# Two cross-attention layers over 16 sequences on one core: turning every probability tile in blocks, with SBUF-to-SBUF exchanges

## The reference

```python
# layer 0: 16 heads of 64
q = x @ Wq + bq;  k = ctx @ Wk + bk;  v = ctx @ Wv + bv
x = layernorm(softmax(q k^T / 8, masked) v @ Wo + bo + x)
# layer 1: 16 heads of 16, self-attention, cross-attention, feed-forward
x = layernorm(x + attention(x q_w, x k_w, x v_w) o_w + o_b)
x = layernorm(x + attention(x cq_w, ctx ck_w, ctx cv_w) co_w + co_b)
x = layernorm(x + relu(x lin1_w + b) lin2_w + b)      # 256 -> 1024 -> 256
```

## Time and profile before

| | before |
|---|---|
| median of 3 runs | 1821.75 us |
| the profiled execution: its own time / its span | 1826.15 / 1824.3 us |
| ScalarE busy | 1190.3 us, 65% |
| GpSimd busy | 990.9 us, 54% |
| data moved by DMA | 324.12 MB, 178 GB/s on average |

### The profile page before, as it was taken

One profiled execution on the slowest core, in us unless ns is written; L12 is line 12 of the kernel. 1 busy time (PEld: TensorE's weight loads), 2 busy tenths in 40 slices (PEclk: granted clock), 3 DMA queues, 4 the chain that ended last, 5 costly groups with the idle time before them and its releaser, 6 DMA issues.

```text
span 1824.3 us, 36986 instructions
## 1 busy us (share of the span) xinstructions
PE 1719.5 (94%) x11328; PEld 1287.7 (71%) x11328; DVE 1269.6 (70%) x4778; ACT 1190.3 (65%) x3985; POOL 990.9 (54%) x1030
## 2 busy tenths in 40 slices
PE   7999999999999999999999999999999999998887
PEld 5776677777777677777777777677777777776556
DVE  3465667786868668686776868678686867667763
ACT  3364766667676666767666676766667677566752
POOL 3252655657465464746556474555657565455742
PEclk9999999999999999999999999999999999998899
DMA  7432327585766758576585757658575766613010
GB/s 167 143 106 84 107 67 230 172 273 161 238 204 200 245 170 272 161 244 206 178 266 181 249 159 236 209 181 280 173 251 163 226 223 182 202 59 139 30 58 12
DMA packets 227521, 324.12 MB, mean 178 GB/s; under 512 B 31744, under 2 KB 196352, under 8 KB 219136
## 3 DMA queue, kind: packets, MB, share of 16 engines
q1 hardware_dynamic: 224208, 321.75, 55.5%
q10 hardware_dynamic: 3120, 0.01, 0.1%
HBM read 170.69 MB, written 151.00 MB: 176 GB/s over the span
## 4 chain that ended last, share of the span: by engine, by line
PE 77%; DVE 6%; DMA 5%; ACT 5%; SPq 5%; issue 2%; POOL 0%; POOLq 0%; DVEq 0%
PE ps_g L681 45%; PE ps_t L824 10%; PE ps_t L847 8%; PE ps_s L800 8%; ACT prob L930 3%; PE ps_av L800 3%; DMA prob_b<-p_kept 3%; PE ps_av L847 3%; DVE prob L1105 2%; DMA p_kept<-blocks 2%; SPq L593 1%; PE ps_g L687 1%; DVE res_ln L1081 1%; DVE prob_b L1136 1%; SPq L576 1%
## 5 line engine op out<-in xcount | busy, mean ns | idle before, releaser
L1229 POOL TENSOR_TENSOR prob<-prob,recip 128x512 f32<-128x512 f32 x768 | 788.4, 1049 | 670.5 <-DVE recip L1115 670.4
L930 ACT ACTIVATE prob<-prob,ext 128x256 f32<-128x256 f32 x1536 | 757.2, 499 | 11.7 <-DVE ext L1105 11.5
L940 ACT ACTIVATE prob_t<-ps_t 128x512 f32<-128x512 f32 x384 | 226.3, 594 | 398.1 <-PE ps_t L824 397.3
L824 PE MATMUL ps_t<-ident,prob 128*128 128x128 f32 x1920 | 304.6, 283 | 7.6 <-DVE prob_b L1136 5.4
L930 ACT ACTIVATION_READ_ACCUMULATOR prob<-prob,ext 128x1 f32 x1536 | 295.5, 192 | 0.0
L824 PEld LDWEIGHTS ps_t<-ident,prob 128*128 128x128 f32 x1920 | 216.9, 142 | 94.2 <-issue 51.6
L1105 DVE CUSTOM_DVE_ANT_0 prob<-ps_s,mask_a 128x256 f32<-128x256 f32 x392 | 145.3, 421 | 88.3 <-PE ps_s L800 70.6
L1127 DVE STREAM_TRANSPOSE blocks<-prob 128x512 f32<-128x512 f32 x288 | 183.9, 676 | 3.2 <-POOL prob L1229 2.3
L1105 DVE CUSTOM_DVE_ANT_0 prob<-ps_s,zero 128x256 f32<-128x256 f32 x392 | 144.4, 418 | 45.3 <-PE ps_av L800 37.3
L1105 DVE CUSTOM_DVE_ANT_0 prob<-ps_s,mask_b 128x256 f32<-128x256 f32 x368 | 135.9, 417 | 24.5 <-PE ps_s L800 14.8
L800 PE MATMUL ps_s<-k_ctx,q 64*128 64x256 f32 x784 | 144.8, 402 | 7.3 <-DVE ext L1105 3.0
(11 more groups left out here) (116 smaller groups left out, 2980.9 us busy)
## 6 DMA issues: line engine op xcount, KB each, us to landing
p_kept<-blocks SPq DMA_DIRECT2D x576, 128.0 KB, 2.4
prob_b<-p_kept SPq DMA_DIRECT2D x144, 512.0 KB, 3.4
k_parts_C<-k_hl SPq DMA_DIRECT2D x64, 256.0 KB, 3.1
k_parts_B<-k_hl SPq DMA_DIRECT2D x64, 256.0 KB, 3.1
q_parts_B<-q_hl SPq DMA_DIRECT2D x64, 256.0 KB, 3.5
k_B<-k_parts_B SPq DMA_DIRECT2D x16, 1024.0 KB, 7.6
q_B<-q_parts_B SPq DMA_DIRECT2D x16, 1024.0 KB, 7.7
q_parts_C<-k_hl SPq DMA_DIRECT2D x64, 256.0 KB, 4.7
```

Of the source, the lines that this page charges most:

```text
L824: last = nc.tensor.transpose(two(ps_t[e])[:, kt, qt * P:(qt + 1) * P], src[:, e, qt, kt * P:(kt + 1) * P], ident[:, :])
L930: last = nc.scalar.activation(tile, tile, ACT.Exp, bias=ext[:, slot, e, t:t + 1], scale=-1.0, accum_out=sums[:, slot, e, t:t + 1])
L940: nc.scalar.activation(prob_t[:, e], two(ps_t[e]), ACT.Copy).then_inc(copied_second, 1)
L1229: nc.gpsimd.tensor_tensor(rows, rows, recip[:, slot, e].unsqueeze(2) .to_broadcast([P, TT, TOK]), ALU.mult).then_inc(normed[s], 1)
```

## The change

1. **All pairs are turned in blocks, in every body.** PE's transposes of `prob`, their PSUM banks and their copies are gone. VectorE turns a pair with one instruction of 128x1024 (step D now at every pair). The keys of a batch are ordered by the host (`ctx_keys`, and the masks with it), or by the way in which the self-attention's keys are read (`keys_out`), so that what lands is in the right order.
2. **A quad's blocks go straight from SBUF to SBUF** (`exchange`): four DMAs, one for each 32 source partitions, when the quad's second pair has been turned. `blocks` holds two quads, `prob_b` three (T_RING), each slot with its own semaphore. LAG is 4, so W comes 5 places after the quad's second pair. `prob` holds three pairs.
3. **PSUM.** The two banks that are free go to the scores, which have four, so PE may be two pairs ahead of VectorE.
4. **q and k of B and q of C are spread from SBUF to SBUF**, in 8 DMAs of 16 partitions each. SP issues k of B; ScalarE issues the queries, four DMAs at step q0 and four at q1. k of C still goes through device memory.
5. **The copy of `v` out of PSUM** goes from VectorE to ScalarE.
6. **Constants** are laid out by the host and loaded in few DMAs; GpSimd no longer sorts weights. A second copy of the context, with ordered keys (`c_k`), is loaded for each batch, 256 KB. `x` is loaded straight into the residual buffer.
7. The jobs stand at other places, and the order of the pairs is AAABBCACBBCC in place of AAABCBACBBCC (in quads).

```diff
-P_RING = 4
-LAG, BLOCKS = 3, 2
+P_RING, B_RING, T_RING = 3, 2, 3
+LAG, BLOCKS = 4, 2
...
         if g - 1 in pairs:
-            steps.append(("R",) + pairs[g - 1][0])
...
+            steps.append(("R",) + pairs[g - 1])
+        if g - BLOCKS in pairs:
+            steps.append(("D",) + pairs[g - BLOCKS])
         steps.extend(jobs)
...
-        ("A", 1): [dma("k", "B"), job("qs"), ln("ln1"), job("v", 0)],
-        ("A", 2): [job("x2T"), dma("q", "B"), job("q", 2), job("qc"), io("value_c")],
...
+        ("A", 2): [job("qs"), dma("k", "B"), ln("ln1")],
+        ("A", 3): [job("x2T"), job("q", 2), dma("q0", "B")],
...
-        prob_b = sb("prob_b", [P, 2, 4, TT * 2 * TT * SLOT])
+        blocks = sb("blocks", [P, B_RING, 4, 2, 2 * TT * TT * SLOT])
+        prob_b = sb("prob_b", [P, T_RING, 4, 2, 2 * TT * TT * SLOT])
...
+            def exchange(body, step):
...
+                quad = body.quad(step)
+                sp.wait_ge(flipped, 2 * quad + 2)
+                if quad >= T_RING:
+                    (_, s0, p0, _), b0 = body.pair_at(2 * (quad - T_RING))
+                    sp.wait_ge(weighed[s0], count(b0, QUADS, p0 // 2 + 1))
                 for q in range(4):
-                    sp.dma_start(by_key[q], blocks[q * SLOT:(q + 1) * SLOT, :, :]).then_inc(spilled, 16)
...
+                    sp.dma_start(prob_b[:, quad % T_RING, q].rearrange("p j x -> p (j x)"),
+                                 blocks[q * SLOT:(q + 1) * SLOT, quad % B_RING].rearrange("r g j x -> r g (j x)")
+                                 ).then_inc(landed[quad % T_RING], 16)
...
+            def spread_keys(b):
+                sp.wait_ge(taken["ks"], count(b, 1, 1))
+                home_free("B", b, "B")
                 for part in range(PARTS):
+                    for e in range(2):
+                        row = HALF * e + DH1 * part
+                        sp.dma_start(k4["B"][row:row + DH1].bitcast(F32), k_hl[:, part % 2, e]
+                                     ).then_inc(spread_k["B"], 16)
...
+                past = body.earlier(step, 2, lambda x: x[0] == "S")
                 if past:
                     (_, s0, p0, _), b0 = past
+                    pe.wait_ge(masked[s0], count(b0, HEADS, 2 * p0 + 2))
...
+            def spread_queries(body, step):
...
+                act.wait_ge((q_high[s], taken["qs" if s == "B" else "qc"])[half], count(b, 1, 1))
+                for part in (2 * half, 2 * half + 1):
+                    for e in range(2):
+                        row = HALF * e + DH1 * part
+                        act.dma_start(q4[home][row:row + DH1].bitcast(F32), parts[:, half, e]
+                                      ).then_inc(spread_q[s], 16)
...
             def extremes(body, step):
...
+                n = body.place(step)
+                if n >= P_RING:
+                    dve.wait_ge(flipped, n - P_RING + 1)
...
             def turn_blocks(body, step):
...
+                if quad >= B_RING and p % 2 == 0:
+                    dve.wait_ge(landed[(quad - B_RING) % T_RING], 64 * ((quad - B_RING) // T_RING + 1))
+                src = prob[:, body.slot(step, P_RING)].rearrange("p e t (k g r) -> p (e t k) g r", k=TT, r=SLOT)
+                out = blocks[:, quad % B_RING, :, p % 2].rearrange("p g (m q) -> p m g q", q=SLOT)
+                nc.vector.transpose(out, src).then_inc(flipped, 1)
```

More of the change, by code:

```diff
@@ L156, in schedule @@
     }
     if present == {"x", "a"}:
-        after = {place: [x for x in jobs if x[1:3] not in (("res0", 0), ("load", 0))] for place, jobs in after.items()}
-        after["A", 0] = [job("k", 1)] + after["A", 0]
-        head += [res("res0", 0), io("load")]
-    if present == {"x"}:
-        first = first[:3]
+        moved = ("res0", 0), ("x_in", 0), ("mask_in", 0), ("v", 2), ("v", 3), ("c_columns", 0)
+        after = {place: [x for x in jobs if x[1:3] not in moved] for place, jobs in after.items()}
@@ L173, in schedule, with last_schedule @@
     if not closed:
-        for _ in range(LAG + 1):
-            line.advance([])
+        for i in range(LAG + 1):
+            line.advance([job("v", 3), io("c_columns")] if present == {"x", "a"} and i == 1 else [])
         steps += here(wo + os + first)
     return steps
-def last_schedule(carried, blocked):
+def last_schedule(carried):
     steps = []
@@ L503, in _, with load_mask @@
         def _(sp):
-            def load(body, step):
+            def load_mask(body, step):
                 b = body.batch(step)
@@ L550, in load_values @@
                              v_kept[bass.ds(b, 1)].rearrange("b p t d -> p b t d")).then_inc(v_loaded, 16)
-            def save_keys(body, step):
-                b = body.batch(step)
-                sp.wait_ge(taken["ks"], count(b, 1, 1))
-                if not (isinstance(b, int) and b == 0):
-                    sp.wait_ge(spread_k["B"], count(b - 1, 16, 16))
-                for part in range(PARTS):
-                    sp.dma_start(k_parts["B"][0, :, part].rearrange("e r c t -> (r c) e t"),
-                                 k_hl[:, part % 2]).then_inc(k_saved["B"], 16)
@@ L695, in columns_out, with keys_out @@
                                    [src[:, d, :] for d in range(DT)])
+                return last
+            def keys_out(ps, w, first, src):
+                for m in range(2):
+                    c = (first + m) * P
+                    last = product(ps[:, m, :].rearrange("p (k g r) -> p k g r", k=TT, r=SLOT),
+                                   [w[:, d, c:c + P] for d in range(DT)],
+                                   [src[:, d, :].rearrange("p (k r g) -> p k g r", k=TT, r=SLOT) for d in range(DT)])
                 return last
@@ L962, in _ @@
                 for step in body.steps:
-                    if step[0] in ("T0", "T1"):
-                        evac_turned(body, step, int(step[0][1]))
-                        continue
+                    if step[0] == "DMA" and step[1] in ("q0", "q1"):
+                        spread_queries(body, step)
                     {"J": job, "X": exps, "AV": evac_weighed}.get(
```

559 lines of the change are left out of this document (219 added, 340 removed).

## The result

The changed kernel takes 2003.11 us, the median of 4 runs (1994.94 to 2012.37), against 1821.38 (1819.41 to 1824.36) of the kernel before on the same chip: 1.099 times as long, with a 95% interval of 1.096 to 1.102. The forecast was 1632 us, faster with a chance of 0.95. The profiled execution has a span of 2010.3 us, 376 us more than the 1634 that were summed up.

What follows compares the result with a forecast made beforehand. PE bounds the kernel; without its turning, PE and VectorE are about level. First part 234, twelve bodies 1152 and last part 248 sum to 1634 us of span, 1632 at the median; 8-in-10 range 1575 to 1705 us.

Steps and rivals of the forecast that it cites:

- The step that failed: Full body: VectorE's 30.9 us in the first stage plus PE's 60.0 in the second, plus 4.3 of waits: 96.0 us.
- The transpose of 1024 elements: VectorE's turning of a pair in one instruction: 1.19 us, no worse than 1.35, for 24 pairs a body.
- ScalarE's 16 issues: DMA issues on ScalarE: 7 to 12 us a body, nothing on the path; without cover, up to 2 us per block of four.
- The spreads: Spreads of k and q of B and q of C: bytes fall from 6 to 3 MB a body.
- The share of 0.90 in the first stage: Busy share of the DMA engines in a body's first stage: should not grow.
- The exchange: A quad's 1 MB in four DMAs: 4 to 11 us from issue to landing, probably 6 to 8.
- the products themselves stay, in number and shape: PE's products: half already read `prob_b` in strided order, so the other half's new order is priced at nothing.
- The clock: PE's granted clock: more falls expected in the last part, 0.94 before; under 0.95 in full bodies would show the forecast wrong.
- The first part (+75): Part before the twelve full bodies: 267.8 us falls to 234, between 226 and 245.
- the last (+55): Part after the twelve full bodies: 274.6 us falls to 248, 236 to 262.
- the first: Rival, 25%: level PE and VectorE hold each other up; a body of 101 us, 1708 us in all.
- the slower one: Rival: exchange landings of 14 us every quad set the pace, about 1838 us; 4% together with any other slower stall.

Runs made afterwards that it cites:

- e1: Changed kernel with the 16 spreads of the queries a body issued by SyncE in place of ScalarE: 1947.57 us.
- e13: Against e1: spreads of k of B and of the queries move 128 bytes of each 1 KB, exchanges stay whole: 1886.36 us.
- e4: Against e1: exchanges move 256 bytes of each 2 KB piece, spreads of k of B and the queries 128 of each 1 KB: 1838.09 us.
- e8: Against e4: the job ks reads its columns straight, not in blocks of keys: 1820.75 us.
- the floor: The kernel of e4, with hardly any bytes in exchanges and spreads: 1838.09 us.
- e11: Against e4: VectorE turns only a quarter of each pair, 256 of 1024 elements: 1781.75 us.
- e16: Against e4: layer norm ln3 of the full bodies at place C6 and its store at C7, in place of B5 and B7: 1827.58 us.
- e9: Against e4: in the full bodies the jobs that PE waited at (x2T, qc, oc, x3T, h, wo) stand one place later: 1846.75 us.
- e12: Against e4: the edits of e8, e9 and e11 together: 1766.00 us.
- m1: Separate kernel without attention that only moves 1 MB at a time, six times each way: exchange 7.1 us, spreads 10.5 us.
- e6: Against e1: each pair exchanged as soon as it is turned, in four DMAs of 128 KB and 1 KB pieces: 2033.36 us.
- e3: Changed kernel with k of B and q of B and C by device memory again, four saves and one load each by SyncE: 2109.78 us.
- e14: Against e1: each exchange DMA moves 2 KB from every partition to the same partition, as many bytes and issues: 1932.09 us.

## Why the prediction was wrong

**The step that failed** is the one that turned stage sums into a body: "a full body then has 30.9 + 60.0 = 90.9 us in the longer engines ... I take 4.3 us [of waits]: 96.0 us". It measured 116.5 us. Over the twelve bodies that is 246 of the 376 us of span:

- *PE's busy time, 1194.8 us instead of 1082: 113 us.* About 70 of it is the clock, an estimate: a granted mean of 0.95 is a tenth of 1398 us at 1.2 GHz, in which half the work is lost if PE was busy throughout; the mean is given to 0.01, which leaves 7 us either way. The strided ks is another 1.89 us a body, 23 us. About 20 are left by subtraction. A turned pair priced too high, at the 1.03 us of the transposes' own rows, would give them; no run shows it.
- *PE's waits, 203 us instead of 70: 134 us.* For spreads 58.8, for the heads of A at wo 48.7, for ctx_C and ctx_B 39.5, for layer norms 32.9, for the exchange 13.8, for q 9.4.

**What the runs put in its place.** In order of removal from 2003: the queries' issues taken off ScalarE 56 us (e1), the spreads' bytes 61 (e13), the exchange's bytes 48 (e4), ks 17 (e8). 189 us remain over 1632 with all of that gone, some 5 of them the clearing at the start. The profile of the floor, which still has the strided ks, divides its own 201 us over the summed span: PE's busy time in the full bodies 79, its waits there 66, the first part 40, the last 16. Of the mechanism behind the waits this much is shown: the longer engine changes every 15 to 35 us (e4's pieces), VectorE's turning is on the path for a fifth of what was taken off it (e11), ln3's place for some 10 us (e16), and shifting PE's jobs alone moves the waits and saves nothing (e9). That the sum of the longer engine over two stages of 34 and 72 us was too coarse follows from the pieces: in the floor, pieces of 50 us miss 114 of the 1276 us that pieces of 5 us show. That a lead of two pairs is too short to level them was only argued; no run had a longer one. What is left of the floor, 134 us in e12, is not settled by a run.

**The other steps, one by one.**

- The transpose of 1024 elements: 1217 ns on average, forecast 1.19 us. VectorE is busy 88.0 us a body, the forecast's 30.9 + 58.1 = 89.0. Right.

```profile
L1025 DVE STREAM_TRANSPOSE blocks<-prob 128x1024 f32<-128x1024 f32 x289 | 351.8, 1217 | 0.6 <-POOL prob L1101 0.3
```

- ScalarE's 16 issues, "I price it at nothing on the path", at most four times 2 us a body: they take 2 to 5 us in a block, and 56 us in all, 3.5 a body, with what the second queue costs in landings. The prices of the earlier trace rows were those of one queue that issues alone; here SyncE issues at the same time. The bound held, the choice within it was wrong. One of the prediction's own signs of being wrong came here: issues of 1.3 us each (5.18 us for four) with VectorE's reciprocals waiting behind them.
- The spreads: priced by bytes, "from 6 to 3 MB", as a gain. They cost 61 us. This is the mis-sized term that I could least have read from the earlier trace rows, in which every save leaves from 128 partitions to device memory. The Trainium skill (SBUF — State Buffer, Door 1: The DMA port swizzle) has the rule that would have priced it: its table gives 16 partitions in a row four ports, by its figure 109 GB/s, an estimate of 9.6 us for 1 MB if the eight pieces go one after another. m1 measured 10.5. I applied that rule to the exchange, where the same reckoning gives 4.8 us and m1 shows 7.1, and not to the spreads.
- "The share of 0.90 in the first stage should not grow": it was 0.91 and then 1.10, with a third less moved.
- The exchange: 4.1 to 4.5 us of issue (up to 5.4 beside ScalarE's) and 4.9 us (median) from an issue to its landing, about 9 us; forecast 4 to 11, probably 6 to 8. W's wait of 1.15 us a body was forecast as under 2, and is right. The forecast watched the right number of the wrong transfer.
- `keys_out` was not priced: "the products themselves stay, in number and shape". The order in which a product reads its columns is not its shape. The Trainium skill (SBUF — State Buffer, Door 1: The DMA port swizzle) states a rule for it: SBUF has lines of 16 bytes, and each access that crosses to a new line pays. A stride of four floats crosses at every element; 3.78 against 1.89 us agrees.
- The clock: 0.85, 0.95 and 0.82 in the first part, the full bodies and the last part, where before it was 0.99, 0.99 and 0.94. The forecast expected some of that in the last part alone. A wait that opens costs again in what follows it, as the row behind ctx_C shows.
- The first part (+75) and the last (+55): 25 of the 75 us are the exchange's bytes (e13, e4) and 40 remain in the floor, and 30 of the 55 are what e1 took away (302.8 against 272.4 us in e1).
- The waits before: "134.6 us on one of the three banks alone" misreads. `ps_s` is two of the three score banks. Nothing in the sum hangs on it.
- The rivals: the nearest in mechanism was the first (level engines that hold each other up), at 1708 us; the slower one named a landing of 14 us a quad, which did not happen. That case had a chance of 0.04 together with any other stall that ends slower. The range ended 300 us too early, because each bound was taken alone: waits up to 10 us a body left out that a late spread, ScalarE's block, a strided read and the clock come on top of one another.

## What to carry to other kernels

Where a change levels two engines, do not sum the longer one over long stages: compare them place by place, and count each crossing as a wait, with the clock behind it. Price every new DMA three times: by the partitions on its narrower side, by what its issue holds up on the engine that issues it (at the rate of two queues that issue at once), and by what is queued behind it. And before changing how work is moved, make a kernel that keeps the issues and moves hardly any bytes: here it takes 1838 us (some 5 of them the clearing) against 1821 to 1825. So with these lists and as many issues there was nothing to win, however good the transfers.

## What the runs showed of the hardware that I had not expected

- From SBUF to SBUF, four issues of 128 pieces each take 2.5 us with pieces of 256 bytes (e4) or 1 KB (e6), but 4.1 us with 2 KB (the changed kernel). Beside ScalarE's issues a single one took up to 2.4 us.
- Two queues at once moved 2 MB in 13.3 us when they started together, where one after the other would take 7.1 + 10.5 = 17.6 us (m1).
- A transfer into 16 partitions is slower from SBUF (10.5 us) than the longer way by device memory (9.0 us); yet in the kernel the way by device memory cost 162 us more than e1, with SyncE waiting 97.7 us for saved queries (e3).
- Products whose columns lie four floats apart take double at full clock: 3.78 us (the changed kernel) against 1.89 (e12) for eight of 128x256.
- A quadrant at the source costs as much as a quadrant on both sides: 7.1 and 7.0 us for 1 MB, against 4.3 from every partition to itself (m1). In the kernel's full bodies the difference did not show (e14).
